# A three-stage decoder layer on one core: shorter norm chain, earlier value weights, reordered last steps, double row buffers

## The reference, cut to what matters

```
x = x + attn(norm(x));  x = x + xattn(norm(x), ctx);  x = x + ffn(norm(x))
attn(r):  y = norm(r)*g + b;  per head of 4: p = relu(y_h @ K.T)**2;  out_h = p @ V;  r + out
xattn:    q = x@Wq, k = ctx@Wk, v = ctx@Wv, 16 heads of 64, 128 keys per batch;
          softmax(mask(q k / 8)) v, merged, @ Wo
ffn:      shared swiglu(x) + the routed expert's swiglu (32 experts, one per token)
```

## Time and profile before

| | |
|---|---|
| three runs | 2864.35, 2863.79, 2860.95 us (median 2863.79) |
| profiled execution | 2861.03 us, of it 2859.4 us from first to last instruction |
| granted TensorE clock, mean | 0.996 |
| stages, by the timeline | self-attention to about 797 us, cross-attention to about 1436, feed-forward with experts to the end |
| PE, DVE, ACT, POOL busy | 97%, 63%, 56%, 36% of the span |

### The profile page before, as it was taken

The page is one execution under the profiler, slowest core; times in us unless marked ns, Lnnn a source line. Parts: engine busy times, 40 slices in busy tenths (PEclk is TensorE's granted clock), DMA queues, the critical chain, the costliest instruction groups (busy, mean ns, idle before and its releaser), DMA issues.

```text
span 2859.4 us, 46307 instructions
## 1 busy us (share of the span) xinstructions
PE 2772.2 (97%) x13287; PEld 2284.7 (80%) x13289; DVE 1804.1 (63%) x2744; ACT 1592.0 (56%) x2744; POOL 1015.1 (36%) x692
## 2 busy tenths in 40 slices
PE   7999999999989999999899999999999999999998
PEld 5888888888778887788778888887788888888886
DVE  6566666666776665667563433435885855676776
ACT  6888888887665554566431111112574744565665
POOL 6888888887522221222200000000232322232332
PEclk9999999999999999999999999999999999999999
DMA  1000000002221102110221111112986964786884
GB/s 63 26 27 11 26 26 26 17 24 70 75 67 45 44 29 59 34 37 28 96 89 59 61 66 60 59 66 87 344 314 216 355 214 146 271 296 228 291 289 175
DMA packets 190791, 322.70 MB, mean 113 GB/s; under 512 B 23528, under 2 KB 49128, under 8 KB 190720
## 3 DMA queue, kind: packets, MB, share of 16 engines
q1 hardware_dynamic: 179440, 296.61, 30.2%
q0 software_dynamic: 11280, 25.20, 2.6%
HBM read 286.86 MB, written 46.66 MB: 117 GB/s over the span
## 4 chain that ended last, share of the span: by engine, by line
PE 86%; DVE 6%; ACT 4%; issue 2%; POOL 1%; ACTq 0%; DMA 0%; DVEq 0%; POOLq 0%
PE d_pG L1977 9%; PE d_pU L1977 8%; PE a_pS L47 4%; PE a_pS L49 4%; PE a_pS L48 4%; PE a_pO L47 4%; PE a_pO L49 4%; PE a_pO L48 4%; PE d_pD L47 3%; PE d_pD L49 3%; PE d_pD L48 3%; PE c_pD L47 2%; PE c_pD L49 2%; PE c_pG L47 2%; PE c_pD L48 2%
## 5 line engine op out<-in xcount | busy, mean ns | idle before, releaser
L157 POOL TENSOR_TENSOR a_pL<-a_p,a_pH 128x1024 fp32r<-128x1024 f32 x256 | 617.8, 2418 | 163.7 <-DVE a_p L348 161.7
L1215 DVE TENSOR_TENSOR e_wL<-e_raw,e_wH 128x1024 fp32r<-128x1024 f32 x384 | 450.3, 1217 | 36.1 <-PE d_pU L1977 24.4
L348 DVE TENSOR_TENSOR a_p<-a_r,a_pS 128x1024 f32<-128x1024 f32 x256 | 312.2, 1220 | 243.4 <-ACT a_r L165 236.2
L1210 ACT CAST e_wH<-e_raw 128x1024 fp32r<-128x1024 f32 x384 | 384.5, 1053 | 86.3 <-PE d_pD L49 59.3
L670 POOL TENSOR_TENSOR b_S<-b_S,b_ri 128x512 f32<-128x512 f32 x128 | 133.2, 1041 | 501.0 <-DVE b_ri L831 501.0
L165 ACT ACTIVATE a_r<-a_pS 128x1024 f32<-128x1024 f32 x256 | 261.8, 1023 | 80.3 <-PE a_pS L49 78.6
L165 ACT ACTIVATE a_pH<-a_r 128x1024 fp32r<-128x1024 f32 x256 | 271.9, 1062 | 9.1
L687 ACT ACTIVATE b_S<-b_S,b_nm 128x128 f32<-128x128 f32 x512 | 198.8, 393 | 35.3 <-DVE b_nm L826 34.7
L1459 POOL DMA_INDIRECT out<-d_og,c_iw x46 | 86.5, 1880 | 359.2 <-DVE d_og L1851 359.2
L47 PE MATMUL a_pS<-a_qH,a_kH 128*128 (+1 forms) x512 | 205.0, 400 | 1.3 <-DVE a_p L348 1.2
L47 PE MATMUL a_pO<-a_pH,a_vH 128*128 128x512 f32 x512 | 199.8, 390 | 1.5 <-POOL a_pL L157 1.5
(11 more groups left out here) (308 smaller groups left out, 7251.2 us busy)
## 6 DMA issues: line engine op xcount, KB each, us to landing
e_raw<-in_L_ffn_routed_gate_w SPq DMA_DIRECT2D x256, 256.0 KB, 4.5
e_raw<-in_L_ffn_routed_up_w SPq DMA_DIRECT2D x256, 256.0 KB, 5.7
e_raw<-in_L_ffn_routed_down_w SPq DMA_DIRECT2D x128, 512.0 KB, 6.8
a_xb<-in_x SPq DMA_DIRECT2D x8, 1024.0 KB, 5.5
x<-a_base SPq DMA_DIRECT2D x32, 256.0 KB, 2.3
b_xr<-x SPq DMA_DIRECT2D x32, 256.0 KB, 3.2
x<-b_xr SPq DMA_DIRECT2D x32, 256.0 KB, 3.0
c_xb<-x SPq DMA_DIRECT2D x32, 256.0 KB, 2.9
```

Source lines behind the costliest of these rows:

```text
L157: nc.gpsimd.tensor_tensor(pL[:, j % RING, :, :], p[:, j % 2, :, :], pH[:, j % RING, :, :].bitcast(F32), ALU.subtract).then_inc(s["low"], 1)
L348: v.tensor_tensor(p[:, j % 2, :, :], r[:, j % 2, :, :], pS[j % 2][:, :, :], ALU.mult).then_inc(s["p"], 1)
L1210: copy(self.wH[n][:, :, :], self.raw[n][:, :, :]).then_inc(self.s["high"], 1)
L1215: unit.tensor_tensor(self.wL[n][:, :, :], self.raw[n][:, :, :], self.wH[n][:, :, :].bitcast(self.F32), self.sub).then_inc(self.s["low"], 1)
```

## The change

1. **Norm chain** (self-attention). r1*r2 is taken as 1/sqrt(v*(1+eps) + eps*eps), so both inverse roots run side by side on 128x2x4 values, with one seed and three Newton rounds: 14 links in place of 29, in 5 parts in place of 9. In group 0 ScalarE first normalizes the 128 columns of the first head of the four tiles (`normalize_first`), then splits the first query, and then does the other 384 columns; PE's first transposes wait for the first part alone.
2. **Value weights.** The high halves of Wv's pieces go from steps 13, 15, 17, 19 to 12, 14, 16, 18, their low halves one step later.
3. **Last two steps of cross-attention** (last group only). VectorE takes t_low ahead of add_mask at j = 6 and 7. Low halves 0 and 1 of the feed-forward weights go to j = 7, between maximum and inverse; 2 and 3 go behind the steps, among the last residual additions.
4. **Two row buffers.** xH and xL exist twice, used in turn by group (`x_part`). The second copy takes the place of the second batch's values. SP stores these (vH and vL of batch 1, 1 MB each) to DRAM (`parked`) between the loads of Wo and the last store of x1, and loads them over the first batch's values in group 4, once values(31) is done (wait on `pv`) and ahead of that group's residual loads; PE waits for them at j = 2. Now norms stand at j = 1 and 3, transposes at the ends of j = 2 and 4, x_high and x_low at j = 3 and 5 (x_low ahead of the norms at j = 3), and every step has its query in its usual place. In group 0 the low halves of Wo move from steps 2, 3, 4, 7 to 2, 4, 6, 7.

A semaphore that nobody waited for is dropped (`warm`), and m_in is renamed mv_in and also counts the parked loads.

```diff
-    LINKS = 29
+    LINKS = 14
...
+        def normalize_first(t, columns, count):
+            scaled(qn[:, t, columns], 0, t, scale, shift, columns).then_inc(s[count], 1)
...
+        act.wait_ge(s["own"], LINKS)
         for t in range(GT):
-            normalize(0, t)
+            normalize_first(t, slice(0, P), "first")
         q_high(0, 0)
+        for t in range(GT):
+            normalize_first(t, slice(P, C), "normed")
...
+            for w in (w2, w2_ps):
+                v.tensor_scalar(w[:, 0, :], mv_ps[:, :, 1], EPS, None, ALU.add)
+                m = v.tensor_scalar(w[:, 1, :], mv_ps[:, :, 1], 1.0 + EPS, EPS * EPS, ALU.mult, ALU.add)
+            link(m)
...
             if part == 0:
                 aggregate(G, link)
-                seed(link, r1_ps, r1)
+                seed(link)
             elif part <= 3:
-                newton(link, r1_ps, r1, var1)
-            elif part == 4:
-                second_variance(link)
-                seed(link, r2_ps, r2)
-            elif part <= 7:
-                newton(link, r2_ps, r2, var2)
+                newton(link)
             else:
-                residual_scales(link)
-        PARTS = 9
+                row_scales(link)
+        PARTS = 5
...
+    parked = [nc.dram_tensor(f"parked{n}", (KEYS, NPAIR, 2, P), F32, kind="Internal").ap() for n in "HL"]
...
-    xH, xL = (at((64 + 8 * i) * KB, n, [P, KC, GTOK], F32R) for i, n in enumerate(("xH", "xL")))
+    xH, xL = (at((40 + 16 * i) * KB, n, [P, 2, (24 - 8 * i) * KB // 4], F32R) for i, n in enumerate(("xH", "xL")))
...
-    W_HIGH_AT = {1: (0, 0), 4: (0, 1), 7: (0, 2), 10: (0, 3), 13: (1, 0), 15: (1, 1), 17: (1, 2), 19: (1, 3),
+    W_HIGH_AT = {1: (0, 0), 4: (0, 1), 7: (0, 2), 10: (0, 3), 12: (1, 0), 14: (1, 1), 16: (1, 2), 18: (1, 3),
...
-    WO_LOW_AT = (2, 3, 4, 7)
+    WO_LOW_AT = (2, 4, 6, 7)
+    X_NORM, X_TURN, X_SPLIT = (1, 3), (2, 4), (3, 5)
...
             for n in range(PIECES):
                 sp.dma_start(raw_o[:, 2 * n:2 * n + 2, :], wo_v[:, 2 * n:2 * n + 2, :]).then_inc(s["wo_in"], 16)
+            sp.wait_ge(s["vL"], 2 * NB)
+            for part, dst in zip((vH, vL), parked):
+                sp.dma_start(dst, part[:, 1, :, :, :].bitcast(F32)).then_inc(s["k_out0"], 16)
             store(g, NH - 1)
...
+            if b > pb:
+                sp.wait_ge(s["pv"], NPAIR * g)
+                for part, dst in zip(parked, (vH, vL)):
+                    sp.dma_start(dst[:, 0, :, :, :].bitcast(F32), part).then_inc(s["mv_in"], 16)
             if not first:
                 outputs(g - 1)
...
-                soon = b > pb and j == 0 or j == NPAIR - 2 and not last
+                soon = b > pb and j == 0 or j >= NPAIR - 2 and last
...
                 maximum(n, j)
-                if j != NPAIR - 2 and not (last and j == NPAIR - 1):
+                if last and j == NPAIR - 1:
+                    aside(j)
+                elif not (last and j == NPAIR - 2):
                     q_low(n + 2, (j + 2) % NPAIR)
...
+                if not last and j in X_SPLIT:
+                    for i in range(2):
+                        x_low(g + 1, 2 * X_SPLIT.index(j) + i)
+                if not last and j in X_NORM:
+                    for i in range(2):
+                        norm(g + 1, 2 * X_NORM.index(j) + i)
                 inverse(n, j, 0)
...
-                if j == NPAIR - 2 and not last:
-                    x_transpose(turn + 2, 2, g + 1)
-                    x_transpose(turn + 3, 3, g + 1)
-                elif j < NPAIR - 2 or j == NPAIR - 1 and not last:
-                    query(n + 2, (j + 2) % NPAIR)
+                if j < NPAIR - 2:
+                    query(n + 2, g, j + 2)
+                elif not last:
+                    if j == NPAIR - 2:
+                        pe.wait_ge(s["xL"], turn + GT)
+                    query(n + 2, g + 1, j + 2 - NPAIR)
...
+                if b > pb and j == 2:
+                    pe.wait_ge(s["mv_in"], 16 + 32)
...
+                if not last and j in X_TURN:
+                    for i in range(2 * X_TURN.index(j), 2 * X_TURN.index(j) + 2):
+                        x_transpose(turn + i, i, g + 1)
...
             x_low(0, 0)
+            w_low(2)
             norm(0, 3)
+            w_low(3)
             out_stats(g, 0)
```

More of the change, by code:

```diff
@@ L249, in aggregate @@
             link(m)
[L250 to L272, removed]
@@ new lines, in aggregate, with both, seed, newton @@
+            link(m)
+        def both(link, op):
+            op(y2_ps)
+            link(op(y2[:, :, :]))
+        def seed(link):
+            link(v.tensor_single_scalar(t2_ps.bitcast(I32), w2_ps.bitcast(I32), 1, op=ALU.logical_shift_right))
+            both(link, lambda out: v.tensor_scalar(out.bitcast(I32), t2_ps.bitcast(I32), -1.0, float(0x5F3759DF), ALU.mult, ALU.add))
+        def newton(link):
+            link(v.scalar_tensor_tensor(out=t2_ps, in0=y2_ps, scalar=-0.5, in1=y2[:, :, :], op0=ALU.mult, op1=ALU.mult))
+            link(v.tensor_tensor(t2_ps, t2_ps, w2[:, :, :], ALU.mult))
+            both(link, lambda out: v.scalar_tensor_tensor(out=out, in0=t2_ps, scalar=1.5, in1=y2[:, :, :], op0=ALU.add, op1=ALU.mult))
@@ L280, in scales, with row_scales @@
+        def row_scales(link):
+            v.tensor_scalar(up[:, :], y2_ps[:, 0, :], 1.0, None, ALU.add)
+            v.tensor_scalar(scale[:, :], y2_ps[:, 1, :], 1.0, None, ALU.mult)
+            for out, y in ((off, y2[:, 0, :]), (shift, y2[:, 1, :])):
+                m = v.scalar_tensor_tensor(out=out[:, :], in0=mv_ps[:, :, 0], scalar=-1.0, in1=y, op0=ALU.mult, op1=ALU.mult)
+            link(m)
         def scales(G, part, link):
@@ L760, in body @@
                 n = NPAIR * g + j
-                if j != NPAIR - 2 and not (last and j == NPAIR - 1):
+                if not (last and j >= NPAIR - 2):
                     q_high(n + 2, (j + 2) % NPAIR)
-                if not last:
-                    for i in {NPAIR - 3: (0, 1), NPAIR - 2: (2, 3)}.get(j, ()):
-                        x_high(GT * g + GT + i, i)
+                if first and j == X_SPLIT[0]:
+                    act.wait_ge(s["k_out0"], 32 * PIECES // 2 + 32)
+                if not last and j in X_SPLIT:
+                    for i in range(2):
+                        x_high(g + 1, 2 * X_SPLIT.index(j) + i)
                 exps(n, j, 0)
@@ L798, in norm, with x_low @@
                                     ALU.subtract, ALU.mult).then_inc(s["normed"], 1)
-        def x_low(t, i):
-            dve.wait_ge(s["xH"], t + 1)
-            at = (slice(None), slice(None), slice(i * P, (i + 1) * P))
-            source = first_pX[i] if isinstance(t, int) and t < GT else pX[i % 2]
-            sub(xL[at], source, xH[at]).then_inc(s["xL"], 1)
+        def x_low(g, i):
+            dve.wait_ge(s["xH"], g * GT + i + 1)
+            source = first_pX[i] if isinstance(g, int) and g == 0 else pX[i % 2]
+            high, low = (x_part(x, g, slice(0, KC), slice(i * P, (i + 1) * P)) for x in (xH, xL))
+            sub(low, source, high).then_inc(s["xL"], 1)
         def q_low(m, j):
@@ L929, in begin @@
             for i in range(GT):
-                x_low(i, i)
+                x_low(0, i)
             q_low(0, 0)
@@ L963, in body @@
                     a_low(n - 2, (j - 2) % NPAIR)
-                if j == NPAIR - 2 and not last:
-                    q_low(n + 2, 0)
-                if j in (1, 6, 7) and last:
+                if j == 1 and last:
                     aside(j)
@@ L998, in x_transpose, with query @@
             m.then_inc(s["xt"], 1)
-        def query(m, j):
+        def query(m, g, j):
             wait(pe, s["qL"], m)
@@ L1122, in body @@
                     p_transpose(n - 1, (j - 1) % NPAIR)
-                if j == NPAIR - 2 and not last:
-                    pe.wait_ge(s["xL"], turn + GT)
-                    query(n + 2, 0)
                 if j == 1 and first:
```

85 lines of the change are left out of this document (38 added, 47 removed).

## The result

The kernel after takes 2825.76 us, the median of four runs (2824.46 to 2826.86), against 2862.37 us for the kernel before (four runs): ratio 0.9869, 95% interval 0.9854 to 0.9884.

A forecast was written before the change was run, and what follows sets the result against it. TensorE, busy 97% of the span, was taken as the bound, so only its idle and half-clock time could be won. 3.7 + 5.0 + 9.0 - 1.0 + 0 + 10 = 26.7 us; median forecast 2837 us, range 2826 to 2848.

The forecast's parts named there:

- Group 0, -1.0: Group 0 of cross-attention under part 4: net 1.0 us lost, between a gain of 3 and a loss of 5.
- so I take 7: SP's queue in group 0: the parked 2.1 MB delay the load of group 1's rows by 7 us, at most 9.9.
- untouched and only starts sooner: Feed-forward stage behind cross-attention (1409 us): the change does not touch it, so no gain was counted.
- Part 2, 5.0: Late part, value weights a step sooner: PE's two waits for low halves of Wv go, 5.0 us (2.5 to 6.1).
- I count 1.1 us lost: Part 2: four newly exposed low halves on VectorE collide with GpSimd's low halves, mostly covered, costing 1.1 us.
- Part 3, 10: Last two steps of cross-attention: waits for t_low and half clock go, a 2.2 us stop comes; 10 us (7 to 12).
- with t_low first the two long waits go: Last two steps of cross-attention: t_low first removes PE's two long waits, 8.4 us, and the half clock, 3.7.
- Plain groups, 9.0: Handovers out of groups 1, 2, 3, 5, 6: 2.9 us of stops go, 1.1 to 1.2 come; 9.0 us (3 to 14.5).
- Part 1, 3.7: Head, norm chain in group 0: PE's first transposes move from 18.94 to 15.2, 3.7 us (1.9 to 4.1).
- the handovers' waits: Rival for plain groups: overruns run into the next step and cancel the 2.9 us; 9 us missing, 2846; chance 0.20.
- the new stops stayed: Rival for plain groups said no new stops: steps with two norms cost nothing, 5 x 1.2 us more won, 2831; chance 0.18.
- a clock under 1.00 inside cross-attention: Sign named as showing the forecast wrong: TensorE's clock below full inside cross-attention.

The follow-up runs named there:

- second profile of after: The kernel after, unchanged, profiled once more; span 2824.2 us against 2822.8 in its first profile.
- the one with later parking: The kernel after with the stores of the second batch's parked values issued behind the loads of group 1's first rows; 2825.30 us.

## Why the prediction was wrong, step by step

The sum was 26.7 us, the spans differ by 36.5 (35.1 with the second profile of after). The waits named for parts 2 and 4 and for the head were the right ones; in part 3 the gain was put down to the wrong move. The missing 8 to 10 us are mostly three terms.

- **Group 0, -1.0, was +2.0 to +2.6.** The failed step is "so I take 7". It scaled the queue's old 11.1 us by bytes, but 2.36 MB in 11.1 us (213 GB/s) was not what the transfers can do: from 784 to 794 us they now move 327 GB/s. The load was 4.8 or 3.9 us late, VectorE waited 1.1 or 0.3 us, and PE's longest stop there is 0.8 or 0.9 us, where 2.8 was forecast. The gains set against it were too small as well: 0.7 and 1.1 us, while PE's waits in the group fell from 3.8 us to 1.7 (1.2 in the second profile).
- **The feed-forward part, counted at nothing, gave 1.1 to 2.8.** The failed step is "untouched and only starts sooner". It was true of the shared part, 530.80 us in all sixteen profiles. But the long wait at the first expert block is followed by full or half clock from run to run, worth 1.4 us, and another 1.1 to 1.4 us is in both profiles of before and in none without its text: the change does touch that stage, by the dropped increment of `warm`, though what brings the gain is open. I should have put 0 to 3 us on it.
- **Part 2, 5.0, was 6.8.** The failed step is "I count 1.1 us lost". Collisions took place, but PE waited for none of them. The other 0.7 us is the half clock with its start, priced at 1.3 and worth 2.0 (6.8 less the waits of 4.8). The rule of the Trainium skill was right about three of the four instructions and says nothing about the path.
- **Part 3, 10, was 10.7**, with the stop of 2.2 (2.0) and the return of full clock as forecast. But "with t_low first the two long waits go" names the wrong move: the low halves' new places do it alone. The walk had both moves in it and never each one. That no half clock was counted behind a stop of 2.2 us rested on one stop of 1.9 us in one trace, and behind that very stop the clock did fall in two other kernels. It fell behind the new stops in none of the eleven profiles that have them; the forecast was right there, but its reason was not.
- **Plain groups, 9.0, were 10.1**: the new stops are there, at j = 4 and 6, but cost 0.8 us a group (2.9 less the 2.1 won) and not 1.1 to 1.2. **Group 4, 0, was 0.2**, since the kernel after has half clock there and the kernel before has none; like for like it was 1.1 (below).
- **Part 1, 3.7, was 3.4 to 4.0**, in part by luck: the normalizing began 2.3 us sooner and not 1.9, its first quarter took 1.64 us and not 1.1. That the other 384 columns "cost nothing" held.
- **The range** (2826 to 2848) took the sum of the good ends (2822) as too unlikely. But part 2 passed its good end of 6.1, and the feed-forward part had no range at all. No rival came true: the handovers' waits did not come back, and the new stops stayed, if shorter. Of the signs of being wrong one did appear, a clock under 1.00 inside cross-attention (0.57, below). It stands behind a stop that every kernel of this case has, and tells nothing of the overruns that it was to show.

## What to carry to other kernels

Where an engine is late, look for side work that stands in front of the critical instruction, and for an idle slot on the same engine to put it in: moving four weight halves was worth 10.8 us here, and moving mask rows and output weight halves 4.2 more by the stages (2.0 by the medians), while reordering the critical instructions was worth nothing beside the first of these moves, and 2.6 us without it. A collision or a late load costs only what exceeds the reserve of the engine behind it; find the wait that would grow before giving it a price. Where a stage holds a long stop of PE, price it with and without half clock behind it, even if the change never touches it.

## What the runs showed of the hardware

Whether the clock falls behind a stop is not fixed by the stop. The handover to the second batch has the same gap, 2.35 us from one transpose to the next, in every kernel; the windows behind it, first of the kernel after, then of the one with later parking:

```profile
1085.00:1089.00 4.00, 4.00 (x17) 3.44 (x16) 3.06 (x5) 3.52 (x14) 1.04 (x1) 0.57 0.01 2
```

```profile
1086.00:1090.00 4.00, 3.72 (x21) 2.88 (x19) 3.10 (x5) 3.75 (x15) 1.04 (x1) 1.00 0.01 2
```

The group took 80.3 us with the fall and 79.4 without: 0.9 us. Of the sixteen profiles, seven have the fall, and its place in the span doesn't tell which: the gap began at 1081.56 in one that has it and at 1081.44 in one that has not. Behind the second stop for b_wL (1.9 us) it cost 1.7 us in two of four profiles, behind the wait at the first expert block 1.4. The shortest stop with a fall behind it was 1.9 us, and one of 2.8 us, in the kernel after, had none. In the head the first relu lies between 20.09 and 21.79 us over thirteen profiles of the same head; in some of these the first score products stand 0.43 us apart in place of 0.23. Against 2.4 us between the four runs of after, that is enough to explain them, though it isn't shown run by run; and a change worth under 3 us can't be read from one profile's end here, only from the marks of the stage it touches.
